# A transformer layer on eight cores: the diagonal scaling matrix of the softmax moved from GpSimd to ScalarE, and the exponentials issued in reversed chunk order

## What is computed

```python
# S = 2048, D = 2048, 16 query heads of 128, one shared key head and value head
q = x @ q_w.T + q_b ; k = x @ k_w.T + k_b ; v = x @ v_w.T + v_b
scores = einsum('bqhd,bkd->bhqk', q, k) / sqrt(128)      # causal mask: -inf above the diagonal
attn = softmax(scores, axis=-1)
a = einsum('bhqk,bkd->bqhd', attn, v) @ o_w.T + o_b
x1 = layernorm(x + a)
y = layernorm(x1 + x1 @ (weight * scale_weight[:, None]).T + bias)
```

## Time and profile before

| | |
|---|---|
| median of 3 runs | 2556.37 us (2555.06 to 2592.63) |
| the profiled execution | 2559.68 us |
| its span on the slowest core | 2558.1 us (cores: 2535.9 to 2558.1 us) |
| PE busy | 1573.7 us, 62% of the span |
| DVE busy | 926.9 us, 36% |
| ACT busy | 817.2 us, 32% |
| POOL busy | 531.6 us, 21% |

### The profile page before, as it was taken

How to read it: one execution, slowest core, us unless ns; L and a number is a source line. 1 busy time by engine, 2 the same in 40 slices (tenths; PEclk the granted TensorE clock), 3 DMA queues, 4 the chain that set the end, 5 groups by cost and what they waited for, 6 DMA issues and landing times.

```text
span 2558.1 us, 26197 instructions; the slowest of 8 cores (2535.9 to 2558.1 us)
## 1 busy us (share of the span) xinstructions
PE 1573.7 (62%) x7216; PEld 722.9 (28%) x7216; DVE 926.9 (36%) x1985; ACT 817.2 (32%) x2014; POOL 531.6 (21%) x655
## 2 busy tenths in 40 slices
PE   0999925555554554545444544545798968969874
PEld 0444412222222222222222222222333323323321
DVE  0000014455544444444444444444115640632444
ACT  0121214444444343334433333343212321312411
POOL 0000013211110000000000000000366525535432
PEclk9999956666666666667566666666899978979986
DMA  9122599000000000000000000000354344354343
GB/s 150 24 42 38 68 109 108 24 1 1 1 1 1 0 1 1 1 1 1 1 1 0 1 1 1 1 1 1 84 173 145 124 144 137 120 166 134 105 134 99
DMA packets 43643, 137.08 MB, mean 54 GB/s; under 512 B 5835, under 2 KB 5868, under 8 KB 42988
## 3 DMA queue, kind: packets, MB, share of 16 engines
q0 software_dynamic: 5296, 34.60, 10.1%
q1 hardware_dynamic: 28988, 84.02, 10.1%
q10 hardware_dynamic: 9216, 16.78, 2.4%
HBM read 153.21 MB, written 33.55 MB: 73 GB/s over the span
## 4 chain that ended last, share of the span: by engine, by line
PE 45%; DVE 16%; ACT 15%; issue 14%; DMA 4%; another core or an unknown queue 3%; POOL 1%; DVEq 1%; ACTq 0%; POOLq 0%; SPq 0%
ACT expS L393 12%; PE psT L259 9%; PE psO L480 8%; DVE mpart L372 8%; PE psT L436 4%; PE psT L826 4%; PE psS L344 3%; PE psT L760 3%; DVE expST L458 3%; PE psU L826 2%; PE psO L826 2%; PE psU L760 2%; DVE ycs L719 2%; DMA wost<-wo_bf 2%
## 5 line engine op out<-in xcount | busy, mean ns | idle before, releaser
L436 PE MATMUL psT<-diagP,expS 128*128 128x128 bf16 x2176 | 271.0, 285 | 672.2 <-DVE expST L458 461.8
L393 ACT ACTIVATE expS<-psS,negm 128x512 bf16<-128x512 f32 (+3 forms) x512 | 314.3, 620 | 553.5 <-DVE negm L376 550.3
L372 DVE TENSOR_REDUCE mpart<-psS 128x1 f32<-128x512 f32 (+3 forms) x512 | 289.7, 603 | 504.1 <-PE psS L353 358.7
L414 POOL TENSOR_SCALAR diagP<-ident_s,rcp 128x128 bf16<-128x128 bf16 x256 | 154.1, 602 | 1323.4 <-DVE rcp L410 1253.0
L436 PEld LDWEIGHTS psT<-diagP,expS 128*128 128x128 bf16 x2176 | 201.6, 130 | 753.4 <-issue 749.7
L480 PE MATMUL psO<-expST,Vsb 128*128 128x512 bf16 x640 | 284.0, 595 | 28.7 <-ACT expST L462 27.9
L344 PE MATMUL psS<-KT,QTO 128*128 128x512 bf16 (+3 forms) x512 | 227.0, 530 | 19.3 <-ACT expS L393 18.9
L458 DVE CAST expST<-psT 128x512 bf16<-128x512 f32 (+1 forms) x320 | 204.1, 638 | 85.5 <-PE psT L436 84.6
L259 PE MATMUL psT<-xTbf,qwst 128*128 128x512 bf16 x1024 | 221.2, 379 | 0.2 <-ACT Vsb L241 0.2
L462 ACT CAST expST<-psT 128x512 bf16<-128x512 f32 (+3 forms) x320 | 160.3, 501 | 149.3 <-PE psT L436 149.3
L405 DVE TENSOR_REDUCE den<-dpart 128x1 f32<-128x2 f32 (+2 forms) x192 | 29.9, 156 | 426.5 <-ACT expS L393 395.9
(11 more groups left out here) (76 smaller groups left out, 1736.1 us busy)
## 6 DMA issues: line engine op xcount, KB each, us to landing
wost<-wo_bf SPq DMA_DIRECT2D x64, 512.0 KB, 4.1
fwst<-fw_bf SPq DMA_DIRECT2D x64, 512.0 KB, 3.2
xres<-xT ACTq DMA_DIRECT2D x64, 256.0 KB, 4.5
outT<-ycs SPq DMA_DIRECT2D x64, 256.0 KB, 3.6
xTbf<-xT POOLq DMA_DIRECT2D x1, 8192.0 KB, 60.0
qwst<-qw POOLq DMA_DIRECT2D x16, 512.0 KB, 5.1
wo_bf<-wo POOLq DMA_DIRECT2D x4, 2048.0 KB, 82.4
fw_bf<-fw POOLq DMA_DIRECT2D x4, 2048.0 KB, 101.2
```

The source lines that it names most:

```text
L372: mc=mcol + kc: e.reduce_max(mpart[:, mc:mc + 1], slot[:, 0:wdt], axis=AX.X),
L393: e.activation(expS8[:, (par * 4 + qt % 4) * S + kc * W: (par * 4 + qt % 4) * S + kc * W + wdt], slot[:, 0:wdt], AF.Exp, bias=negm8[:, nco ...
L414: ncol=ncol: e.tensor_scalar(diagP[:, (par * 4 + j) * 128:(par * 4 + j + 1) * 128], ident_s[:], rcp8[:, ncol:ncol + 1], None, AluOpType.mult),
L436: qt=qt: e.matmul(bk[:, i * 128:(i + 1) * 128], expS8[:, (par * 4 + qt % 4) * S + kt * 128: (par * 4 + qt % 4) * S + (kt + 1) * 128], diag ...
```

## The change

The diff makes three edits in `sc_soft`. The wait of the negated maximum names all exponentials of the tile two heads earlier instead of the last one. The exponentials run over the chunks in reversed order, so that the masked chunk comes first. And `diagP` is made by ACT (an Identity activation with `rcp8` as its scale) instead of POOL, so its event now counts on semaphore `a` instead of `p`.

```diff
                     negm8[:, ncol:ncol + 1], mpart[:, mcol:mcol + nkc],
                     axis=AX.X, negate=True),
-                    waits=mx_all + [E_expl2[par][j]], inc="v")
+                    waits=mx_all + E_exall2[par][j], inc="v")
                 E_ex = None
                 ex_all = []
-                for s, slot, wdt, kc, E_mm in chunks:
+                for s, slot, wdt, kc, E_mm in reversed(chunks):
...
-                E_diag2v[par][j] = p.op("gpsimd", lambda e, par=par, j=j,
-                                        ncol=ncol: e.tensor_scalar(
+                E_diag2v[par][j] = p.op("scalar", lambda e, par=par, j=j,
+                                        ncol=ncol: e.activation(
                     diagP[:, (par * 4 + j) * 128:(par * 4 + j + 1) * 128],
-                    ident_s[:], rcp8[:, ncol:ncol + 1], None,
-                    AluOpType.mult),
-                    waits=[E_rq, E_trmm2[par][j]], inc="p")
+                    ident_s[:], AF.Identity,
+                    bias=0.0, scale=rcp8[:, ncol:ncol + 1]),
+                    waits=[E_rq, E_trmm2[par][j]], inc="a")
```

## The result

The changed kernel takes 1.013 times the time of before (95% interval 1.0116 to 1.0144): eight runs gave 2587.67 to 2647.19 us, median 2611.54. The other four lie between 2588 and 2592 us; the prediction was 2588. With 2556.4 before, that is 32 us or 1.2 to 1.3% more. When the changed kernel was run again, on another occasion, it had a median of 2588.4 us over six runs, but the kernel before, run beside it, had 2563.3, and the ratio was 1.0092.

The account below looks back on a forecast made before the run. No engine was near full in attention; chains of handoffs closing each block's loop were taken as the bound. Terms +29.2 + 9.7 - 3.8 - 3.8 = +31.3 us on the median 2556.4 gave 2588 us, range 2562 to 2617.

Parts of the forecast that it names:

- What an activation for `diagP` costs: On ACT, making `diagP` takes 0.39 us, bounds 0.27 and 0.60, and DVE's handoff to ACT 0.10 us.
- The removed wait: Without the satisfied wait on POOL, DVE gains 0.06 us per tile whose loop runs through `den` and `rcp`; bounds 0 and 0.12.
- Block 2, the term that decides: In attention block 2, ACT's cast behind `diagP` delays PE's third group 1.04 us, 30 times; block +29.2 us net.
- Block 0: In attention block 0, the cast of `j` = 3 comes 0.77 us late, 15 times; block +9.7 us net.
- the tile with about 0.1 us to spare: In block 0, at `j` = 1, `diagP` and a cast just fit into ACT's wait for DVE's maximum.
- Block 1: In attention block 1, the 1.04 us before ACT's cast hides in idle time averaging 2.09 us; block -3.8 us.
- Block 3: In attention block 3, ACT's later cast is covered by PE's matmuls with 0.07 us to spare; block -3.8 us.
- The rest: Reversed order (bounds 0 and +8 us), longer wait list, POOL's moved memsets and the function table cost nothing.
- the dearer `diagP`: Rival: `diagP` takes 0.60 us and its handoff 0.23, opening block 3 too; +34 us on top, 2622 us; chance 0.11.
- The clock: Rival: 20 more of 128 iterations of blocks 2 and 3 run at 2.4 GHz, returning 32 us; 2556 us; chance 0.08.
- ACT's casts were not what PE waited for: Rival: in block 2 another event released PE, so that block loses nothing; 2554 us; chance 0.04.
- The tables: Rival: two function table loads per tile on ACT, +657 us, 3210 us; chance below 1 in 100.

Follow-up runs that it names:

- the late `diagP`: Changed kernel, same instructions, but `diagP` issued on ACT behind the next iteration's casts; ratio 0.9930 to the kernel before, two executions, 2540.8 and 2548.1 us.
- the larger dose: Changed kernel with `diagP` written twice on ACT, the second time behind a wait on the first; median 2642.1 us, ratio 1.0303 to the kernel before.

## Why the prediction was right

The time was right to a microsecond (2588 against a median of 2588.05), and so was each block's sign. The mechanism is shown; that the number was met so closely is luck. Block 2 grew by 4.4 us more than forecast, block 1 shrank by 2.4 more, the rest of the profiled execution was 4.8 shorter for no cause in the change, and against the kernel before as it ran on the second occasion the change cost 25 us and not 31. By the steps:

- *What an activation for `diagP` costs*: 0.39 forecast, 0.401 measured; the handoff from `rcp` 0.10 forecast, 0.10 measured (1508.65 to 1508.75).
- *The removed wait*: 0.06 forecast, 0.07 measured, and shown by its own run. Too small by a sixth: some 2 us in all. The Trainium skill ("Advanced Engine Details and Errata", Network/Comms) gives 50 to 100 ns for reading a semaphore; the measured 0.07 us lies in that span, in its middle and not at its lower end.
- *Block 2, the term that decides*: the cast 0.93 us behind the row sum, measured 0.93. A turn that ends with a tile whose group 0 is on ACT grew from 7.11 to 8.13 us (that tile being `j` = 1) and from 6.09 to 7.11 (`j` = 3), medians of steps 3 to 14 on all cores: 1.02 against 1.04 forecast. 30 waits were counted in windows that cut the block a little short; there are 32 of both kinds, which adds 2 us to the forecast. The block grew by 33.6 and not 29.2 on the profiled core, by 34.4 in the mean of the cores. What is left, 2 to 3 us, fits the clock, which the term left out: in 31 of the 96 turns from `j` = 2 to `j` = 3 PE had over a tenth of its busy time at 2.4 GHz in the kernel before, and these took 5.74 us on average; in the changed kernel this happened in none of 96, and all took 7.11 or 7.12. In the profiled cores the same 192 matmuls with V took 86.8 us instead of 83.6:

```profile
752.00:1209.00 457.00, 83.59 (x192) 23.63 (x192) 0.64 0.00 1
```

```profile
756.00:1247.00 491.00, 86.78 (x192) 24.50 (x192) 0.61 0.00 1
```

The size of this part is small beside the 11 us by which the cores of the kernel before differ in block 2, and no run isolates it. That the place in ACT's order is the cause, and not ACT's load, is shown by the late `diagP`.

- *Block 0*: forecast 9.7, measured 10.4. A step grew from 8.01 to 8.63 us, 0.62 where the forecast has 0.77 - 0.12 = 0.65. So the tile with about 0.1 us to spare held in the changed kernel. The larger dose, 0.49 us of it, made a step 0.76 longer; that the 0.27 beyond the dose are this tile's fits, and no run takes it apart.
- *Block 1*: hidden, as forecast, and -6.2 instead of -3.8. The means of the cores give -5.3, and the step, 15.43 to 15.16 us, gives 4.3 for sixteen of them; one core differs from another by 2 us here.
- *Block 3*: cover of 0.07 us forecast, 0.09 found by the larger dose. -4.7 instead of -3.8, by the size of the wait.
- *The rest*: the reversed order and the longer list at nothing, shown.

Of the rivals, the dearer `diagP` was the near one. It was not the case, at 0.401 us. The larger dose is that case made real: 2642 us for 0.50 us more, and block 3 opened as the rival said it would from 0.07 us on. Its handoff of 0.23, from `rcp` to POOL, holds a second, satisfied wait besides (see the end), which ACT doesn't have. The clock did not take the cost back. The prediction called a granted clock that differs a sign of being wrong, and it does differ: 0.63 to 0.58 in block 0 and 0.63 to 0.61 in block 2, means of the cores. Block 0's steps came out as forecast all the same, and in block 2 it went against the kernel, by a few microseconds. That ACT's casts were not what PE waited for is refuted by the late `diagP`, which gave the time back by letting them go first. The tables never came in.

What was not seen at the time of the prediction stands in the same rows. The chain of block 3 ran from exponentials through `den` and `rcp` to a cast that depends on neither. The prediction priced what the change adds to such a queue and not what the kernel already lost in it, which was more than ten times as much (some 420 us, with what the clock added, against 32).

## What to carry to other kernels

When an instruction is moved to an engine with idle time, what counts is what stands behind it in that engine's order: 0.40 us of work cost 1.04 us per turn where it put a long wait ahead of a cast, and nothing where it stood behind that cast. Look for the same pattern in the kernel as it is: an evacuation queued behind an unrelated wait holds the producer's bank, and issuing it earlier gave a sixth of this kernel's time, together with the higher clock that came with it. A wait that is always satisfied still costs (0.07 us here) if it is issued behind the one that comes last; where another wait implies it, leave it out.

## What the runs showed of the hardware

- A satisfied wait on VectorE between the event that comes last and the next instruction costs 0.07 us: 0.17 us from the row sum to the total with it, 0.10 without, as the median of the 64 tiles in each of blocks 1 to 3, and the same from the row sum to the reciprocal in block 0. On ScalarE the exponential starts 0.095 us behind the negated maximum with one wait (200 times) and 0.150 with two (56 times).
- The handoff from VectorE's reciprocal to the next engine took 0.095 us to ScalarE. To GpSimd (`rcp` to `diagP` before) it took 0.166 us in the 8 tiles with one wait and 0.227 in the 248 with a second one, on TensorE's semaphore, behind it. So the move also shortened that step, in part by a wait that ScalarE doesn't need. No block's loop was seen to run through it: with the wait on GpSimd left out, the steps of blocks 1 and 3 are 15.16 and 38.63 us with `diagP` on either engine.
- TensorE's granted clock changed with the order of other engines' work. With the casts ahead of the exponentials it was 0.80 in block 3 instead of 0.66; with group 0 on ScalarE it was 0.54 to 0.60 on the cores in block 2 instead of 0.62 to 0.64, where PE had the same matmuls to do in a shorter time. The fall was not expected, and its cause is open.
- The kernel before had medians of 2556, 2562, 2564 and 2563 us on four occasions (the last three on three chips), the changed one 2588 us on both of its own. The same pair gave ratios of 1.0130 and 1.0092. Whether chip or occasion makes the difference wasn't settled.
